# Splitting two attentions' weights in the feed-forwards ahead of them, with identity products and the first routed tiles' loads placed anew

## The chip, the cores and the metric

One Trainium2 chip, one of its cores. The metric is the device time of one execution of the whole program in microseconds (us), the median over several runs. The engines are TensorE (PE, with PEld for its weight loads), VectorE (DVE), ScalarE (ACT), GpSimd (POOL) and SyncE (SP, which here only issues transfers).

## What is computed

Eight sublayers in a row, each added to its input x (8 x 256 tokens of 256 numbers, all float32), with a context of 8 x 256 rows of 192:

```python
x = x + cosine_attention(layernorm(x), ctx, ...)       # L0 attention
x = x + moe_gelu(layernorm(x), ...)                    # L0: 2 shared + 16 routed experts, top 4
x = x + cross_attention(layernorm(x), ctx, heads=16)   # L1
x = x + bitlinear_silu(layernorm(x), ...)              # L1: ternary weights
x = x + cross_attention(layernorm(x), ctx, heads=8)    # L2
x = x + small_experts(layernorm(x), ...)               # L2: 8 experts, top 2
x = x + text_image_attention(layernorm(x), ctx, ...)   # L3: ternary weights, two attentions
x = x + routed_ffn(layernorm(x), ...)                  # L3: 8 experts, top 2

def cross_attention(x, context, Wq, Wk, Wv, Wo, bo):   # DIM_HEAD 64, SCALE 64 ** -0.5
    q, k, v = x @ Wq, context @ Wk, context @ Wv
    attn = softmax(q k^T * SCALE)                      # per head
    return (attn v) @ Wo + bo
```

## The kernel before

The program is a row of stages, each one block of five instruction streams (one per engine) that work against each other through semaphores. A block ends with a drain of every engine and a barrier, so no engine begins the next stage before the last has finished this one. The stages are `l0_cosine` (L380), `l0_ffn` (L648), `cross_attention` (L980) as l1x with 16 heads, `l1_ffn` (L1488), `cross_attention` as l2x with 8 heads, `l2_ffn` (L1711), `text_side` (L2039), `place_and_route` (L2377) and `routed_tiles` (L2639). Tokens stand in 16 tiles of 128; X holds them all in SBUF.

**Precision by splitting.** In the first feed-forward and both attentions a float32 product is made from two rounded parts: high = value rounded to F32R, low = value − high, and hi·hi + lo·hi + hi·lo on PE. The weights Wq, Wk and Wv are split once at the start of each attention block: ACT copies them to the high part (`hi_part`, L1210; the query's with the factor 64^-0.5), DVE makes the low part by one scalar_tensor_tensor (`lo_part`, L1301). In l1x an instruction covers 128x1024, in l2x 128x512, two for each weight. PE's first projection ("qk", 0) (L1103, L1106) waits for `wqk_lo` 4; the first value product ("v", 0) (L1131) for `wv_lo` 2. POOL zeroes the missing rows of wk and wv (L1444) and splits the context (`context(b)`, L1421 to L1426), adds the output bias to X (`bias`, L1441) and later divides by the row sums (L1434) and splits Wo (L1457). DVE's order at the start is: the norm's factors, all due `normalise(b)` (L1309, two tiles each), lows of Wq and Wk, `low_x(0)` (L1313), lows of Wv. PE's is: identity products, transposes of x(0) (L1092), identity products, qk(0).

**Where raw weights come from.** `K.raw` (8192 float32 columns) is shared: `load_attention_weights` (L917) fills it by SP. For l1x this stands in `l0_ffn`, behind the ternary quantiser's waits; for l2x at the end of l1x's SP stream.

**l0_ffn.** 18 experts by 4 chunks of 512 tokens are 72 units n. For each unit PE makes `hidden(n+1)` and `outputs(n)`, ACT the gelu (L819) and the high part (L823), DVE the low part (L855, `h − h_hi`, both in SBUF) and four scaled additions to X (L864). POOL splits each expert's weights four units ahead (L706 to L710) and between them makes ternary weights for later stages (`TernaryWeights.step`, L347 to L359). The last four units also make the next norm's statistics (L159).

**Identity products.** `keep_running(pe, K, bank, n)` (L98) issues n products of the identity, 128x256 in bfloat16, whose results are not used. The counts in the kernel before: l0_cosine 28 ahead of the sum; l0_ffn 26 at the start; the attentions 60 or 32 at the start and 44 behind x(0); l1_ffn 76; l2_ffn 28 at the start and 14 in `outputs(0, 0)`; routed_tiles 20.

**The last stage.** `routed_tiles` takes 39 tiles of 128 token slots. SP reads a tile's first row from `tile_row` (value_load) and loads its rows from DRAM (`slots`) into an area of XT; `place_and_route` before it writes the tables with DVE and scatters the tokens' rows with POOL's indirect transfers.

## Time and profile before

| | us |
|---|---|
| three runs | 1607.03, 1601.3, 1602.35 (median 1602.35) |
| the profiled execution | 1607.3 |
| its span, first to last instruction | 1605.6 |
| mean granted clock of TensorE | 0.974 |
| PE, DVE, ACT, POOL busy | 1473.8, 970.5, 772.7, 634.0 |

The granted clock is a share of 2.4 GHz: 1.00 is that, 0.50 is 1.2 GHz. All times below are from the span's start in the profiled execution. "Rows ready" is the end of the instruction that makes the last of the rows that the first transposes read; "products end" is where the identity products of the start give way to the first transposes.

| stage | begins | rows ready | products end |
|---|---|---|---|
| l0_cosine | 3.3 | 10.8 | none |
| l0_ffn | 68.7 | 71.8 | 74.0 |
| l1x | 315.0 | 319.2 | 323.8 |
| l1_ffn | 714.4 | 722.6 | 724.3 |
| l2x | 799.9 | 804.1 | 803.6 |
| l2_ffn | 1032.1 | 1035.5 | 1036.9 |
| text_side | 1138.2 | | |
| place_and_route | 1235.4 | | |
| routed_tiles | 1309.2 | | 1313.1 |

In a timeline row the columns are start, duration (of the whole group where there are several), engine, line, operation, output<-inputs, shapes, count, and in brackets the idle time before it with what ended it. L94 and L2414 as releaser are the barrier between two stages.

### The profile page before, as it was taken

The page shows a single profiled execution, that of the slowest core. Times are in us where ns is not written, and L with a number is a line of the kernel's source. Part 1 is how long each engine was busy: PE and PEld are TensorE (multiplying, and loading weights), DVE is VectorE, ACT ScalarE, POOL GpSimd, SP SyncE. Part 2 cuts the span into 40 slices and gives each one's busy share as a digit, 9 for nine tenths or more (in the row PEclk, how much of TensorE's full clock was granted, in tenths as well). Part 3 has the DMA queues.
Part 4 walks back from the last instruction along what each step waited for, and adds up shares of the span by engine and source line. Part 5 has one row for each costly group of instructions (what it writes and reads, how often), then busy time and mean ns, then how long its engine had stood idle before and what let it go on. Part 6 is the DMA issues. An engine that isn't in the chain of part 4 may idle for free. (4 is left out here: it accounts for less than half of the span.)

```text
span 1605.6 us, 29383 instructions
## 1 busy us (share of the span) xinstructions
PE 1473.8 (92%) x9850; PEld 1177.7 (73%) x9871; DVE 970.5 (60%) x2369; ACT 772.7 (48%) x1907; POOL 634.0 (39%) x828
## 2 busy tenths in 40 slices
PE   6799999899999999978899999789889859999997
PEld 4588888787777777755577767557565649999997
DVE  3768888865555555557866656455587634444443
ACT  2643444465555555526556565343558523434332
POOL 0138999463444443234365544001432432222212
PEclk9999999899999999999999999999999779999999
DMA  9000122309600000010000000100500842222220
GB/s 292 21 14 21 32 94 102 119 12 311 189 1 1 1 1 1 1 40 1 4 14 1 1 2 12 68 0 1 224 34 28 295 148 34 37 36 36 37 38 8
DMA packets 69266, 92.97 MB, mean 58 GB/s; under 512 B 7160, under 2 KB 60416, under 8 KB 68224
## 3 DMA queue, kind: packets, MB, share of 16 engines
q1 hardware_dynamic: 61968, 82.55, 16.4%
q0 software_dynamic: 7152, 8.55, 3.1%
q8 instruction: 83, 1.36, 0.3%
q14 instruction: 63, 0.52, 0.1%
HBM read 56.35 MB, written 35.63 MB: 57 GB/s over the span
## 5 line engine op out<-in xcount | busy, mean ns | idle before, releaser
L1434 POOL TENSOR_SCALAR XT<-XT,l1x_rs 128x256 f32<-128x256 f32 x256 | 118.1, 482 | 190.6 <-DVE l1x_rs L1318 190.6
L2699 POOL DMA_INDIRECT out_x<-XT x39 | 60.7, 1557 | 235.6 <-DVE XT L2795 233.6
L1322 DVE TENSOR_REDUCE l1x_nmax<-bank 128x2 f32<-128x512 f32 x128 | 87.4, 684 | 109.5 <-PE bank L1141 109.5
L1261 ACT ACTIVATE XT<-bank,l1x_nmax 128x256 f32<-128x256 f32 x256 | 118.9, 472 | 68.5 <-DVE l1x_nmax L1322 68.4
L2722 PEld LDWEIGHTS bank<-XT,l3x_qw 128*128 128x128 f32 x1248 | 145.3, 192 | 3.3 <-issue 0.7
L2722 PE MATMUL bank<-XT,l3x_qw 128*128 128x128 f32 x1248 | 145.8, 275 | 1.0 <-issue 0.5
L2734 PE MATMUL bank<-l3x_wd,CT 128*128 x624 | 141.0, 379 | 0.0
L1153 PE MATMUL bank<-ident,XT 128*128 128x128 f32 x768 | 120.8, 280 | 7.5 <-DVE l2x_pt L1329 3.5
L2734 PEld LDWEIGHTS bank<-l3x_wd,CT 128*128 128x128 f32 x624 | 115.6, 190 | 14.1
L864 DVE SCALAR_TENSOR_TENSOR X<-bank,l0f_gates,X 128x256 f32<-128x256 f32 x288 | 118.8, 473 | 3.0 <-PE bank L784 3.0
L100 PE MATMUL bank<-ident,identb 128*128 128x256 bf16 x616 | 85.8, 305 | 31.8 <-PEq L2414 17.5
L1153 PEld LDWEIGHTS bank<-ident,XT 128*128 128x128 f32 x768 | 84.3, 140 | 41.2 <-POOL XT L1434 20.9
L1329 DVE COPY l1x_pt<-bank 128x512 f32<-128x512 f32 x128 | 87.9, 686 | 30.5 <-PE bank L1153 30.5
L2770 ACT ACTIVATE CT<-bank,l3x_b 128x128 f32<-128x128 f32 x156 | 44.7, 368 | 125.4 <-PE bank L2722 125.3
L819 ACT ACTIVATE l0f_h<-bank 128x512 f32<-128x512 f32 x72 | 43.1, 599 | 127.7 <-PE bank L766 127.7
L100 PEld LDWEIGHTS bank<-ident,identb 128*128 128x128 bf16 x616 | 66.1, 109 | 47.5 <-issue 33.7
L2814 DVE TENSOR_SCALAR CT<-bank,l3x_b 128x128 f32<-128x128 f32 x156 | 44.1, 344 | 89.1 <-PE bank L2722 89.0
L782 PE MATMUL bank<-l0f_wdhi,l0f_hhi 128*128 128x256 f32 x288 | 83.0, 288 | 9.2 <-DVE l0f_hlo L855 9.1
L855 DVE TENSOR_TENSOR l0f_hlo<-l0f_h,l0f_hhi 128x512 fp32r<-128x512 f32 x72 | 67.6, 939 | 33.6 <-ACT l0f_hhi L823 33.2
L1434 POOL TENSOR_SCALAR XT<-XT,l2x_rs 128x256 f32<-128x256 f32 x128 | 59.1, 484 | 69.7 <-DVE l2x_rs L1318 69.2
L784 PE MATMUL bank<-l0f_wdhi,l0f_hlo 128*128 128x256 f32 x288 | 81.9, 284 | 0.0
L783 PE MATMUL bank<-l0f_wdlo,l0f_hhi 128*128 128x256 f32 x288 | 81.7, 284 | 0.0
(531 smaller groups left out, 3826.4 us busy)
## 6 DMA issues: line engine op xcount, KB each, us to landing
slots<-blank SPq DMA_DIRECT2D x9, 1987.5 KB, 21.4
l3x_wu<-in_L_ffn_W SPq DMA_DIRECT2D x8, 1024.0 KB, 12.9
l3x_wd<-in_L_ffn_W SPq DMA_DIRECT2D x8, 1024.0 KB, 8.8
XT<-slots SPq DMA_DIRECT2D x39, 132.5 KB, 2.1
l0f_wu<-in_L_ffn_upT SPq DMA_DIRECT2D x18, 128.0 KB, 2.1
l0f_wd<-in_L_ffn_downT SPq DMA_DIRECT2D x18, 128.0 KB, 2.2
X<-in_x SPq DMA_DIRECT2D x4, 512.0 KB, 5.5
l0x_later<-in_L_xattn_W_f1T SPq DMA_DIRECT2D x1, 2048.0 KB, 12.0
```

Of the source, the lines that this page charges most:

```text
L100: pe.matmul(bank[:, 0:2 * P], K.identb[:], K.ident[:].bitcast(BF16), start=True, stop=True)
L782: pe.matmul(y, h_hi[:, c % 2, w], wd_r[s][0][:], start=True, stop=False)
L783: pe.matmul(y, h_hi[:, c % 2, w], wd_r[s][1][:], start=False, stop=False)
L784: last = pe.matmul(y, h_lo[:, c % 2, w], wd_r[s][0][:], start=False, stop=True)
L864: dve.scalar_tensor_tensor(X[:, t, :], YB[c % 2 * 2 + j // 2][:, j % 2 * D:(j % 2 + 1) * D], gates[:, t, e:e + 1], X[:, t, :], ALU.mult, A ...
L1153: last = pe.transpose(tp[:, c:c + P], pr[n % 3][:, i, q, kt * P:(kt + 1) * P], K.ident[:])
L1261: act.activation(pr[n % 3][:, i, q, :], sc[(2 * n + i) % 3][:, q * S:(q + 1) * S], ACT.Exp, bias=nmax[:, n % 3, i, q:q + 1], accum_out=sum ...
L1322: dve.tensor_reduce(nmax[:, n % 3, i, :], sc[(2 * n + i) % 3][:].rearrange("p (q s) -> p q s", q=QT), AX, ALU.max, negate=True).then_inc(m ...
L1329: dve.tensor_copy(pt[n % 2][:, i, :], tp[:]).then_inc(pt_ok, 1)
L1434: pool.tensor_scalar(t, t, rs[:, n % 3, i, q:q + 1], 1.0, ALU.mult, ALU.mult).then_inc(norm_ok, 1)
L2722: last = pe.matmul(up_b[i % 2][half][:, j * P:(j + 1) * P], chosen[i % 2][:, k, m * P:(m + 1) * P], xT[i % 2][:, k, :], start=k == 0, stop ...
L2734: last = pe.matmul(y_b[i % 2][:, 0:D], hT[i % 2][:, m, :], wd[:, ds(e * HT + m, 1), :].rearrange("p a n -> p (a n)"), start=m == 0, stop=m ...
```

## The change

`load_attention_weights` gives way to a class `AttentionWeights`. One buffer `wqkv` of 8192 F32R columns, shared by both attentions, holds the high and low parts: Wq and Wk of l1x (Wv of l1x has a buffer of its own and is still split in l1x), all three of l2x. The query's weights are scaled in place by ACT, then copied to the high part; the low part is a subtraction on POOL in place of DVE's instruction. l1x's Wq and Wk are split in `l0_ffn`, l2x's weights in `l1_ffn`. In the attention block DVE now does `normalise(0)` and `low_x(0)` first and the other due tiles afterwards.

```diff
+class AttentionWeights:
+    def __init__(self, K, name):
+        self.parts = [[K.wqkv[:, (2 * i + part) * 2 * HD:...].rearrange("p (k n) -> p k n", n=HD) for part in range(2)]
+                      for i in range(min(3, WQKV // (4 * HD)))]
+        self.cuts = [slice(0, 1), slice(1, 2)] if HD == 1024 else [slice(0, 2)]
+    def scale_query(self, act, u):
+        act.wait_ge(self.raw_in[0], self.raw_n[0])
+        act.activation(self.raw[0][:, cut, :], self.raw[0][:, cut, :], ACT.Copy, scale=self.scale).then_inc(self.scaled, 1)
+    def high(self, act, i, u):
+        act.wait_ge(...)
+        act.activation(self.parts[i][0][:, cut, :], self.raw[i][:, cut, :], ACT.Copy).then_inc(self.hi_ok, 1)
+    def zero_rows(self, pool, i):
+        pool.memset(self.parts[i][1][HALF_C:P, 1, :].bitcast(F32), 0.0).then_inc(self.zeroed, 1)
+        pool.wait_ge(self.zeroed, i)
+    def low(self, pool, i, k):
+        pool.wait_ge(self.hi_ok, n * i + (k if n == 2 else 0) + 1)
+        pool.tensor_tensor(self.parts[i][1][0:rows, k, :], self.raw[i][0:rows, k, :],
+                           self.parts[i][0][0:rows, k, :].bitcast(F32), ALU.subtract).then_inc(self.lo_ok, 1)
```

In `l0_ffn` (POOL before its first split, POOL at its end, PE, ACT behind `hidden(n)`; N is 72):

```diff
+                if K.last >= 2:
+                    K.weights["l1x"].zero_rows(pool, 1)
                 pool.memset(gates[:, :, 0:NS], 1.0).then_inc(ones_ok, 1)
                 split(0)
...
+                    for i in range(2):
+                        for k in range(2):
+                            K.weights["l1x"].low(pool, i, k)
...
+                    if n == N - 1:
+                        keep_running(pe, K, bank[3], 15)
...
-                keep_running(pe, K, bank[4], 26)
+                keep_running(pe, K, bank[4], 30)
...
+                keep_running(pe, K, bank[3], 28)
...
+                    if K.last >= 2 and N - 10 <= n < N - 8:
+                        K.weights["l1x"].scale_query(act, n - (N - 10))
+                    elif K.last >= 2 and N - 8 <= n < N - 4:
+                        K.weights["l1x"].high(act, (n - (N - 8)) // 2, n % 2)
```

In `cross_attention` (PE, ACT, DVE, POOL):

```diff
-                keep_running(pe, K, tp, 60 if H == 16 else 32)
+                keep_running(pe, K, tp, 36 if H == 16 else 26)
...
                         if u == ("x", 0):
-                            keep_running(pe, K, tp, 44)
+                            keep_running(pe, K, tp, 14)
...
+                keep_running(pe, K, tp, 24 if H == 16 else 16)
...
                 norm.scalar(act)
-                act.wait_ge(K.raw_loaded, K.raw_needed[name])
-                for k in range(KD):
-                    hi_part(raw_q, wq, k, DH ** -0.5)
-                for k in range(2):
-                    hi_part(raw_k, wk, k)
+                if late_v:
+                    for k in range(2):
+                        weights.high(act, 2, k)
                 copy(("x", 0))
-                for k in range(2):
-                    hi_part(raw_v, wv, k)
...
-                for b in range(B):
-                    if turn_at.get(b, -3) - 1 <= -2:
+                normalise(0)
+                low_x(0)
+                for b in range(1, B):
+                    if turn_at[b] - 1 <= -2:
                         normalise(b)
-                for k in range(KD):
-                    dve.wait_ge(w_hi, k + 1)
-                    lo_part(raw_q, wq, k, wqk_lo, DH ** -0.5)
-                for k in range(2):
-                    dve.wait_ge(w_hi, 2 + k + 1)
-                    lo_part(raw_k, wk, k, wqk_lo, rows=HALF_C if k else P)
-                low_x(0)
-                for k in range(2):
-                    dve.wait_ge(w_hi, 4 + k + 1)
-                    lo_part(raw_v, wv, k, wv_lo, rows=HALF_C if k else P)
...
-                for w in (wk, wv):
-                    pool.memset(w[1][HALF_C:P, 1, :].bitcast(F32), 0.0).then_inc(w_zero, 1)
-                pool.wait_ge(w_zero, 2)
+                if late_v:
+                    weights.zero_rows(pool, 2)
                 context(0)
+                if late_v:
+                    for k in range(2):
+                        weights.low(pool, 2, k)
                 context(1)
                 bias(0)
```

In `l1_ffn` (POOL behind `lift_hidden(t)`, ACT at the end of tile t):

```diff
+                    for i in (1, 2):
+                        K.weights["l2x"].zero_rows(pool, i)
...
+                    if K.last >= 4 and 9 <= t < 15:
+                        K.weights["l2x"].low(pool, (t - 9) // 2, (t - 9) % 2)
...
+                    if K.last >= 4 and t == 2:
+                        K.weights["l2x"].scale_query(act, 0)
+                    elif K.last >= 4 and t in (4, 5, 6):
+                        K.weights["l2x"].high(act, t - 4, 0)
```

The other identity products: `l0_cosine` gets 34 ahead of its first transposes, 52 for 28 ahead of the sum and 10 behind it; `l1_ffn` 70 for 76; `l2_ffn` 14 more in `outputs(1, 0)`; `place_and_route` 44 at its end; `routed_tiles` 6 for 20. To make room, the ternary quantisers of the first two stages write over the raw values (`later`) and into XT in place of buffers of their own. The loads of the first two tiles' rows move from `routed_tiles` to the end of `place_and_route`'s SP stream, and the last table instruction of DVE signals SP:

```diff
+                sp.wait_ge(tables_ok, 1)
+                sp.wait_ge(scattered, 16 * NT * k)
+                first_tiles(sp)
                 sp.wait_ge(K.stored, 16 * NC)
...
-                load(0)
-                load(1)
                 sp.dma_start(b2.rearrange("p e d -> p (e d)"), b2_src.partition_broadcast(P)).then_inc(b2_in, 16)
-                for i in range(2, SLOT_TILES):
+                for i in range(tile_rows.EARLY, SLOT_TILES):
...
-                keep_running(pe, K, bank[7], 20)
+                keep_running(pe, K, bank[7], 6)
                 turn_input(0)
```

## Rows read from the trace of the kernel before

**Rows 1.** The page, part 1: busy time and share, instructions
```profile
PE 1473.8 (92%) x9850; PEld 1177.7 (73%) x9871; DVE 970.5 (60%) x2369; ACT 772.7 (48%) x1907; POOL 634.0 (39%) x828
```

**Rows 2.** Timeline of PE, 305 to 331: start, length, line, shape, idle before and releaser
```profile
315.08 8.84 PE L100 MATMUL bank<-ident,identb 128*128 128x256 bf16 x60 [4.18 <-PEq L94]
...
324.19 4.97 PE L100 MATMUL bank<-ident,identb 128*128 128x256 bf16 x44
328.92 0.49 PE L1103 MATMUL bank<-l1x_xhi,l1x_wqhi 128*128 128x256 f32 x2
```

**Rows 3.** Timeline of DVE, 303 to 331
```profile
317.08 2.17 DVE L1309 TENSOR_SCALAR XT<-X,l1x_small 128x256 f32<-128x256 f32 x2
319.17 2.89 DVE L1301 SCALAR_TENSOR_TENSOR l1x_wqlo<-raw,l1x_wqhi 128x1024 fp32r<-128x1024 f32 x2
321.99 3.99 DVE L1301 SCALAR_TENSOR_TENSOR l1x_wklo<-raw,l1x_wkhi 128x1024 fp32r<-128x1024 f32 x2
```

**Rows 4.** Timeline of PE, 798 to 815
```profile
799.97 3.65 PE L100 MATMUL bank<-ident,identb 128*128 128x256 bf16 x32 [1.84 <-PEq L94]
...
811.09 0.48 PE L1103 MATMUL bank<-l2x_xhi,l2x_wqhi 128*128 128x256 f32 x2 [1.50 <-DVE l2x_xlo L1313]
```

**Rows 5.** Timeline of DVE, 798 to 813
```profile
806.15 1.81 DVE L1301 SCALAR_TENSOR_TENSOR l2x_wqlo<-raw,l2x_wqhi 128x512 fp32r<-128x512 f32 x2
```

**Rows 6.** Windows: stretch, busy us of PE, PEld, DVE, ACT, POOL, granted clock
```profile
309.20:319.50 10.30, 6.12 (x31) 4.48 (x29) 8.89 (x26) 4.45 (x6) 4.22 (x5) 0.50 0.10 14
319.50:323.70 4.20, 4.20 (x41) 3.76 (x39) 4.20 (x3) 0.84 (x1) 4.04 (x3) 1.00 0.00 0
...
796.00:804.00 8.00, 4.80 (x41) 3.76 (x40) 4.48 (x14) 4.60 (x8) 3.75 (x5) 1.00 0.08 18
...
1097.70:1104.50 6.80, 6.80 (x25) 4.97 (x23) 1.69 (x10) 0.21 (x1) 2.16 (x4) 0.50 0.00 1
1295.70:1312.80 17.10, 3.53 (x17) 2.55 (x18) 3.21 (x8) 1.06 (x1) 6.72 (x7) 0.50 0.23 76
```

**Rows 7.** Groups by line and form, POOL subtractions and additions, mean ns
```profile
L1441 POOL TENSOR_TENSOR X<-X,l2x_bo 128x512 f32<-128x512 f32 x8 | 10.6, 1319 | 16.9 <-DVE XT L1309 16.8
...
L2628 POOL TENSOR_TENSOR X<-X,l3t_shift 128x1024 f32<-128x1024 f32 x4 | 9.3, 2375 | 26.1 <-DVE l3t_shift L2608 26.1
```

**Rows 8.** Line L1210, by source: ns of one, first and last start
```profile
L1210 ACT ACTIVATE l1x_wqhi<-raw x2: 1039/1040/1040, 316.5 to 317.4; 128x1024 fp32r<-128x1024 f32 x2
```

**Rows 9.** DMA issues from 268 to 296: KB each, us to landing
```profile
raw<-in_L_xattn_Wq SPq DMA_DIRECT2D x1, 1024.0 KB, 10.3
```

**Rows 10.** Timeline of ACT, 270 to 283
```profile
282.07 0.60 ACT L819 ACTIVATE l0f_h<-bank 128x512 f32<-128x512 f32 x1 [2.03 <-PE bank L766]
```

**Rows 11.** Timeline of DVE, 278 to 296
```profile
277.25 1.58 DVE L855 TENSOR_TENSOR l0f_hlo<-l0f_h,l0f_hhi 128x512 fp32r<-128x512 f32 x1 [0.56 <-ACT l0f_hhi L823]
...
283.37 0.69 DVE L855 TENSOR_TENSOR l0f_hlo<-l0f_h,l0f_hhi 128x512 fp32r<-128x512 f32 x1 [0.30 <-ACT l0f_hhi L823]
```

**Rows 12.** Timeline of POOL, 278 to 296
```profile
276.13 2.15 POOL L359 TENSOR_TENSOR l0f_back_q<-l0f_back_above,l0f_back_q 128x1024 bf16<-128x1024 bf16 x1
```

**Rows 13.** Timeline of PE at the seams and at two waits
```profile
17.92 2.08 PE L445 MATMUL bank<-CT,l0x_wt 128*128 128x512 f32 x2 [0.64 <-DMA CT<-in_ctxT]
...
68.72 5.42 PE L100 MATMUL bank<-ident,identb 128*128 128x256 bf16 x26 [1.75 <-PEq L94]
...
308.56 0.36 PE L782 MATMUL bank<-l0f_wdhi,l0f_hhi 128*128 128x256 f32 x1 [1.81 <-DVE l0f_hlo L855]
...
714.35 10.12 PE L100 MATMUL bank<-ident,identb 128*128 128x256 bf16 x76 [3.02 <-PEq L94]
...
1032.14 4.88 PE L100 MATMUL bank<-ident,identb 128*128 128x256 bf16 x28 [2.50 <-PEq L94]
...
1095.72 0.67 PE L1815 MATMUL bank<-l2f_b,l2f_weT 8*128 8x256 f32 x2 [1.65 <-DVE X L1987]
...
1309.27 4.03 PE L100 MATMUL bank<-ident,identb 128*128 128x256 bf16 x20 [17.54 <-PEq L2414]
```

139 lines of the change are left out of this document (85 added, 54 removed).

## The prediction, made before the changed kernel was run

> **What bounds the kernel now.** I read the page first: TensorE (PE) is busy 92% of the span [rows 1]. So time is gained only where PE waits, where it works at the low clock, or where it works on identity products while real work could have begun. The timeline at the seams of the stages shows the last. At the start of the first attention PE runs 60 and then 44 identity products, and the first projection of queries and keys starts at 328.92, 13.9 us after the block begins [rows 2]. In that time VectorE (DVE) normalises two tiles and then splits weights for 2.89 + 3.99 us before it may touch the queries' rows [rows 3]. The second attention has the same picture at half the width: its first projection is at 811.09, 11.2 us in [rows 4], with a split of 1.81 us for one weight and a like one for the next [rows 5]. The windows give the clock: 0.50 (1.2 GHz) in stretches behind seams, 1.00 (2.4 GHz) otherwise [rows 6].
>
> **The sum** is made against the profiled execution (1607.3 us, span 1605.6), which is 5.0 us over the median of 1602.35. A measurement of this kernel can tell about 0.5% (8 us) from no change.
>
> 1. *First attention's start: −7.3.* Without the splits DVE's normalise ends at 317.08 + 2.17 = 319.25 [rows 3]. Four transposes (0.6), ScalarE's (ACT) copy (0.6) and DVE's low part (0.7) put the first projection at about 321.4 against 328.92 [rows 2]: −7.5. The 36 products need 36 × 0.11 = 4.0 us at the full clock, so they end at 319.0, before the rows are there; 14 behind the transposes take 1.5, about the length of copy and low part. GpSimd (POOL) now also makes the value weights' low parts between its two first contexts, so its second context and the bias wait behind them: 2 × 2.4 us by the nearest row [rows 7], which makes the first value product at worst 2 us late. Bounds −8 and −5.
> 2. *Second attention's start: −4.9.* All four tiles were normalised ahead of the split (802.4 to 806.2); now two are, and the first projection falls at 804.3 + 1.9 = 806.2 against 811.09 [rows 4]. Two weights' splits leave the path [rows 5]. Bounds −5.5 and −4.
> 3. *Where the first attention's splits go: the first feed-forward, +2.3.* Six ACT instructions of 1.04 us [rows 8] stand behind the last units' activations. A unit takes 2.82 us, of which ACT works 1.23, so one instruction of 1.04 fits. But the first waits for Wq, issued at 271.75 and landing 10.3 us later [rows 9], at 282.05; it stands behind the activations of 278.8 and just ahead of those of 282.07 [rows 10], which are held for 1.0 us. I take +0.5 (0 to +1.1), PE having a unit in hand. POOL's four low parts of 128x1024, 2.375 us each by the nearest row of that size [rows 7], follow its last split at 293.84. DVE's subtraction with both inputs in SBUF (L855) takes 0.69 us alone and 1.58 beside a POOL subtraction: the one that starts at 277.25 ends at 278.83, and POOL's, of 2.15 us, ran from 276.13 to 278.28 [rows 11, 12]: DVE's waited for POOL's end and then ran. With low parts back to back a unit can't be shorter than 2.375 + 0.69 = 3.07 us, +0.25 for each of four; where DVE comes badly it is 0.9, as in rows 11. I take four of 0.45, +1.8. Bounds 0 and +7.6 (four whole low parts less DVE's half us of slack each). The Trainium skill, "SBUF — State Buffer", section "Who interferes with whom", says that a Vector instruction with two SBUF inputs contends with a GpSimd one that reads SBUF, and that the second to issue blocks until the first is done; the trace agrees, with 0.89 us lost behind 2.15. Taken strictly it allows the bad end of that bound.
> 4. *The first feed-forward's end: −0.9.* PE waits 1.81 us before the last output block, whose products then run at half clock from 309.2 [rows 13, 6]; 15 products (1.65 us) fill the wait. DVE's tail of statistics allows no end before 313.3 against 314.2. The 28 products behind the block end before that.
> 5. *Second attention's splits, in the second feed-forward: +0.5.* That stage is bound by DVE, whose work there reads PSUM or one SBUF tensor; ACT has gaps of 1.4 us between activations for its four instructions of 1.04, and POOL is idle for 43 us in all ahead of its quantisations. Each of six low parts of 128x512 at 1.32 [rows 7] can delay one of them. Bounds 0 and +1.5 by these gaps; with nothing hidden it is 4 × 1.04 + 6 × 1.32 = 12.1, which rival C takes.
> 6. *Seams.* In the table of seams the rows are ready before the identity products end. First feed-forward: 26 ran at half clock for 5.42 us from 68.72 [rows 13], and the transposes began at 73.98 though the rows were there at 71.8; at full clock 30 take 3.3. POOL's split of the first weights ends at 74.6 whatever PE does, so −1.0, and +0.3 for 10 products ahead of the seam: −0.7. Second: 76 took 10.12 from 714.35 [rows 13], rows ready at 722.6: −1.7, and +0.5 for 24 products that end behind DVE: −1.2. Third: 28 took 4.88 from 1032.14 [rows 13], rows ready at 1035.5: −1.0 (0 to −1.2).
> 7. *Third feed-forward's middle: −3.3.* PE waits 1.65 us until 1095.72 [rows 13]; from 1097.7 to 1104.5 the clock is 0.50 with PE never idle [rows 6]: 6.8 us at half speed, 3.4 lost. 14 products fill 1.54 of the wait. Bounds 0 and −3.4.
> 8. *The cosine's start: −1.5.* 34 products from 3.4 us on can raise the clock before the first rows, but the context lands only at 17.92 [rows 13], so PE then waits longer for it and the clock may fall again. From 17.92 to 32.8 PE works without a stop at half speed, 14.9 us, so the ends are 0 and −7.
> 9. *Last stage's start: −0.7.* 20 products took 4.03 us [rows 13] ahead of the first transposes; now 6 do, and the first tile's rows are loaded under POOL's drain. The real products come up to 2.4 us sooner, but at 0.50, where the clock rose at 1312.8 before [rows 6]. Bounds −2.4 and +1.
> 10. *At nothing:* the query scaled in place (the same ACT lengths, in a feed-forward); the ternary weights in other buffers; 44 products behind the routing, in a wait of 17.54 us [rows 13]; two loads of about 1 us to issue moved on SP's queue behind the stores, where nothing else is queued; SP's wait for the tables, whose last step ends before POOL's scatters. If POOL's drain didn't cover the loads, they'd cost 2 us, the bound of term 9.
>
> Sum: −7.3 − 4.9 + 2.3 − 0.9 + 0.5 − 0.7 − 1.2 − 1.0 − 3.3 − 1.5 − 0.7 = −18.7, so 1588.6 against 1607.3, or 1583.7 from the median. The 5 us between the runs shown are most likely clock; then the median run lacks some of the falls that 7 and 8 take back, and I put 1.3 back: 1585, −1.1%.
>
> **Rivals.**
> *A, the clock holds in the cosine (0.18).* Term 8 is −6 or −7: 1580. For it: PE's waits there are short once the context is in [rows 13]. Against: the wait for the context becomes some 3 us.
> *B, products don't hold the clock where they now stand (0.12).* PE idles of 1.81 and 1.65 us were followed by falls [rows 13, 6], one of 1.84 at 799.97 was not (1.00 from 796 to 804 [rows 4, 6]), so a short idle decides by its place. Fewer products then leave real work at half clock: terms 4, 6, 7 and 8 near nothing, 9 at +1, 1 at −5.5: sum about −6, 1596. The Trainium skill speaks for it, "TensorE: Matmul & The Clock Gate", Part 4: transpose-mode work does not count as busy in the same way. These are plain matmuls with the identity, and the row of 60 raised the clock by itself, 0.50 until 319.5 and 1.00 after [rows 2, 6]; the trace speaks against that rule for them.
> *C, slower (0.04).* The splits land on in-order queues in full stages. If each ACT instruction (10 × 1.04), the low parts by their bound (7.6) and the six of 1.32 are on the path, that is 25.9 in place of 2.8 counted, and the clock terms 4 and 6 to 9 (9.3) need not come: −18.7 + 23.1 + 9.3 = +13.7, 1616 from the median. It decides once the moved work costs over 21 us. Against it: ACT's wait for PE of 2.03 us before 282.07 [rows 10].
> *D, the splits' terms alone come (0.04):* −7.3 − 4.9 + 2.8 = −9.4, 1593.
> The forecast has 0.62.
>
> The range is 1576 to 1597: A less 4 for the bounds of 1 to 3, B plus 1. Faster by over 0.5% is below 1594.3: the forecast, A, most of D, a little of B: 0.85. Same 0.12, slower 0.03.
>
> **What would show it.** First projections some 6.3 us into both attentions; no DVE instruction that reads raw query, key or value weights; L855 slowed beside just four POOL low parts, the last of which ends before the stage does; one hidden activation about 1 us late at Wq's landing; clock 1.00 across the seams of term 6 and from 1097.7 to 1104.5; the middles of both attentions unchanged. I'd be wrong if units with an added instruction grew by its full length, or if falls of the clock only moved to the next real work.

## The result, and the profile after

The changed kernel takes 1598.06 us (median of seven runs, 1596.54 to 1602.27) against 1604.57 for the kernel before (seven runs, 1601.3 to 1610.65): a ratio of 0.996, 95% interval 0.9944 to 0.9975. That is 6.5 us where 17 were forecast (1585). The profiled execution has a span of 1600.5 us against 1605.6, so the profiles show 5.1 of these 6.5 and the stages can be set beside each other. Each column is one execution (the changed kernel's, at 1602.27 us, is the slowest of its seven), and what a stage does in other executions of the same code comes further down.

| stage | before | after | forecast change | change |
|---|---|---|---|---|
| l0_cosine | 65.4 | 65.9 | −1.2 | +0.5 |
| l0_ffn | 246.4 | 251.1 | +0.4 | +4.7 |
| l1x | 399.3 | 395.9 | −6.8 | −3.3 |
| l1_ffn | 85.6 | 85.6 | −1.2 | 0.0 |
| l2x | 232.2 | 229.6 | −4.9 | −2.6 |
| l2_ffn | 106.1 | 102.7 | −4.3 | −3.4 |
| text_side | 97.1 | 97.7 | 0 | +0.6 |
| place_and_route and routed_tiles | 370.2 | 368.7 | −0.7 | −1.5 |

(Stages are counted from the first busy instruction of one to that of the next; the last from 1235.4 and 1231.8 to the end.)

The page's row of busy time, which answers to [rows 1], says nothing of it:

```profile
PE 1478.2 (92%) x9953; PEld 1183.4 (74%) x9974; DVE 962.3 (60%) x2357; ACT 774.6 (48%) x1907; POOL 649.9 (41%) x840
```

Two stages come near what was forecast, the third feed-forward and the last. Both attentions give half of it, and the first feed-forward loses 4.7. I began with the first attention. DVE's timeline there:

```profile
321.30 1.30 DVE L184 TENSOR_TENSOR l1x_small<-l1x_small 128x16 f32<-128x16 f32 x1
322.88 0.25 DVE L186 RECIPROCAL l1x_small<-l1x_small 128x16 f32<-128x16 f32 x1 [0.28 <-ACT l1x_small L191]
323.17 0.25 DVE L187 SCALAR_TENSOR_TENSOR l1x_small<-l1x_small 128x16 f32<-128x16 f32 x1
323.45 3.31 DVE L1354 TENSOR_SCALAR XT<-X,l1x_small 128x256 f32<-128x256 f32 x2
328.14 0.69 DVE L1358 TENSOR_TENSOR l1x_xlo<-bank,l1x_xhi 128x512 fp32r<-128x512 f32 x1 [1.38 <-ACT l1x_xhi L1274]
```

In [rows 3] the normalise of two tiles took 2.17 us; it takes 3.31 now, and one of the norm's small instructions (L184, 128x16) takes 1.30, where it took 0.18 in the kernel before. POOL beside it:

```profile
320.26 0.95 POOL L976 MEMSET l1x_wvlo<- 64x1024 f32 x1 [11.31 <-POOLq L94]
321.29 1.28 POOL L1458 TENSOR_TENSOR l1x_chi<-CT,zero 128x512 fp32r<-128x512 f32 x1
322.65 0.74 POOL L1460 TENSOR_TENSOR l1x_clo<-CT,l1x_chi 128x256 fp32r<-128x256 f32 x1
323.46 0.73 POOL L1463 TENSOR_TENSOR l1x_chi<-CT,l1x_chi 64x256 fp32r<-64x256 f32 x1
324.27 2.34 POOL L983 TENSOR_TENSOR l1x_wvlo<-raw,l1x_wvhi 128x1024 fp32r<-128x1024 f32 x1
```

The instruction L184 starts at 321.30, just behind the start of POOL's context subtraction at 321.29, and ends at 322.60, when POOL's is done (322.57). In the kernel before two memsets of wk and wv stood in front of that context; one has gone with the change, the other is still there, and POOL's first context begins 1.0 us in where it began 1.9 us in. The normalise then runs beside POOL's third context instruction and the first low part of Wv, which the change had put there: its second tile starts with the low part, at 324.27, and ends at 326.76, 0.15 us behind the low part's end. PE shows what comes of it:

```profile
320.30 4.09 PE L100 MATMUL bank<-ident,identb 128*128 128x256 bf16 x36 [1.79 <-PEq L94]
326.82 0.66 PE L1146 MATMUL bank<-ident,XT 128*128 128x128 f32 x4 [2.43 <-DVE XT L1354]
327.31 2.52 PE L100 MATMUL bank<-ident,identb 128*128 128x256 bf16 x14
329.49 0.78 PE L1157 MATMUL bank<-l1x_xhi,wqkv 128*128 128x256 f32 x2
```

The first projection is 9.2 us behind the block's start, not 13.9 and not the 6.3 forecast, and it begins at the low clock: PE waited 2.43 us for the rows, and from 328.0 the windows have 0.50.

Windows of the changed kernel, with columns as in [rows 6]:

```profile
7.10:17.40 10.30, 5.01 (x30) 3.01 (x27) 9.46 (x38) 1.50 (x4) 0.00 (x0) 1.00 1.06 295
17.40:31.00 13.60, 13.01 (x39) 8.79 (x40) 1.58 (x5) 4.76 (x9) 0.00 (x0) 0.50 1.06 368
...
85.70:89.10 3.40, 3.40 (x16) 3.40 (x17) 2.00 (x3) 0.00 (x0) 0.95 (x1) 0.50 0.06 19
133.40:136.80 3.40, 3.40 (x14) 3.10 (x14) 2.92 (x8) 0.00 (x0) 0.00 (x0) 0.51 0.00 0
328.00:331.40 3.40, 3.40 (x19) 2.94 (x17) 0.69 (x1) 0.11 (x1) 3.24 (x4) 0.50 0.00 0
715.40:718.80 3.40, 2.56 (x24) 2.33 (x25) 1.24 (x9) 1.50 (x2) 1.48 (x3) 1.00 0.52 148
727.40:730.80 3.40, 2.84 (x7) 1.24 (x9) 0.00 (x0) 2.58 (x4) 3.29 (x7) 0.50 0.00 0
...
1094.00:1104.50 10.50, 10.39 (x59) 7.86 (x57) 4.43 (x18) 2.07 (x5) 2.15 (x4) 1.00 0.01 2
```

The other rows of this view say where the clock went: 1.00 from 1094 to 1104.5, as forecast; 1.00 early in the cosine, then 0.50 while it works behind the wait for the context; new falls at 85.7 and at 133.4 in place of those of the kernel before, at 66.9 and at 121.5; and at the second feed-forward's start the fall only moved, from the identity products (715.4) to the real ones (727.4). The seams of [rows 13] look as forecast in PE's timeline, a wait filled and transposes soon behind the products:

```profile
1031.42 3.22 PE L100 MATMUL bank<-ident,identb 128*128 128x256 bf16 x28 [0.95 <-PEq L94]
1034.86 1.09 PE L1820 MATMUL bank<-ident,l2f_xn 128*128 128x128 f32 x8 [0.22 <-DVE l2f_xn L1991]
```

and in the third feed-forward:

```profile
1092.99 1.69 PE L100 MATMUL bank<-ident,identb 128*128 128x256 bf16 x14
1094.80 0.67 PE L1866 MATMUL bank<-l2f_b,l2f_weT 8*128 8x256 f32 x2
```

In the second attention the norm is slowed in the same way: both memsets are gone from POOL's front, its context starts with the block, L179 takes 1.21 in place of 0.18, and the first projection comes 8.3 us in (11.2 before, 6.3 forecast). The first two normalises take 1.68 us, as before.

DVE's timeline at the second attention's start:

```profile
801.90 1.21 DVE L179 TENSOR_TENSOR l2x_small<-stats 128x16 f32<-128x16 f32 x1
803.04 0.17 DVE L180 TENSOR_TENSOR l2x_small<-stats 128x16 f32<-128x16 f32 x1
...
804.04 0.69 DVE L184 TENSOR_TENSOR l2x_small<-l2x_small 128x16 f32<-128x16 f32 x1
...
806.11 1.68 DVE L1354 TENSOR_SCALAR XT<-X,l2x_small 128x256 f32<-128x256 f32 x2
```

One profile doesn't price a stage. The experiments below leave several stages as they are in one kernel or the other, so each gives such a stage once more (us; for the second and third feed-forwards, all kernels with the old and with the new counts):

| stage | with the old code or counts | with the changed kernel's |
|---|---|---|
| l0_cosine | 65.4, 65.4, 65.2, 62.1 | 65.9, 65.9, 65.9, 63.7, 63.5, 63.4 |
| l0_ffn | 246.4, 246.7 | 251.1, 249.4, 249.4, 247.9 |
| l1_ffn | 85.6, 85.6, 85.7, 85.4 | five of 85.5 or 85.6, five of 84.0 or 84.1 |
| l2_ffn | 106.1, 106.2, 106.2, 102.9 | ten of 102.7 to 103.2 |

In the second feed-forward the two values part by the clock: the five of 85.5 and 85.6 each have a fall of 3.4 us that begins 10.9 to 11.7 us into the stage, the five of 84.0 and 84.1 have none. The table's +4.7 for the first feed-forward is the worst of four, and its +0.5 for the cosine lies within what the same code does.

### The profile page after: what moved, and what is told of

Read it like the earlier page. It is cut to its first block and busy times, and to the rows that moved or that the text cites. A ratio compares the mean times of both kernels' runs of the same rounds, so it can differ in the third digit from the quotient of the medians.

```text
span 1600.5 us, 29590 instructions
## 1 busy us (share of the span) xinstructions
PE 1478.2 (92%) x9953; PEld 1183.4 (74%) x9974; DVE 962.3 (60%) x2357; ACT 774.6 (48%) x1907; POOL 649.9 (41%) x840
## 5 line engine op out<-in xcount | busy, mean ns | idle before, releaser
L2804 PEld LDWEIGHTS bank<-l3x_wd,CT 128*128 128x128 f32 x624 | 115.6, 190 | 14.1
L100 PE MATMUL bank<-ident,identb 128*128 128x256 bf16 x719 | 91.2, 286 | 26.0 <-PEq L2466 15.3
L100 PEld LDWEIGHTS bank<-ident,identb 128*128 128x128 bf16 x719 | 72.3, 103 | 39.8 <-issue 28.6
L793 PE MATMUL bank<-l0f_wdhi,l0f_hhi 128*128 128x256 f32 x288 | 83.3, 289 | 11.5 <-DVE l0f_hlo L871 11.4
## 6 DMA issues: line engine op xcount, KB each, us to landing
l3x_wu<-in_L_ffn_W SPq DMA_DIRECT2D x8, 1024.0 KB, 13.9
```

The lines of the kernel that those rows point to most:

```text
L100: pe.matmul(bank[:, 0:2 * P], K.identb[:], K.ident[:].bitcast(BF16), start=True, stop=True)
L793: pe.matmul(y, h_hi[:, c % 2, w], wd_r[s][0][:], start=True, stop=False)
L2804: last = pe.matmul(y_b[i % 2][:, 0:D], hT[i % 2][:, m, :], wd[:, ds(e * HT + m, 1), :].rearrange("p a n -> p (a n)"), start=m == 0, stop=m ...
```

## The experiments

All are measured beside the kernel before, in five rounds; ratios are to it. Where two intervals overlap, a difference of medians between two of these kernels isn't settled by the times alone, and the profiles have to carry it. These theories stood at first. **C**: POOL's earlier subtractions block DVE's instructions for their whole length. **P or S**: the loss comes from the identity products placed anew, or from the splits in the first feed-forward.

### The two halves of the change alone

e1_products_old: the changed kernel with every count of identity products as before (13 places).

```diff
-                keep_running(pe, K, bank[7], 34)
-                keep_running(pe, K, bank[0], 52)
+                keep_running(pe, K, bank[0], 28)
...
-                keep_running(pe, K, tp, 36 if H == 16 else 26)
+                keep_running(pe, K, tp, 60 if H == 16 else 32)
```

> The changed kernel with every count of identity products as in the kernel before; splits and early loads stay. Theory P (the products placed anew cost more at the first feed-forward's start than they bring at other seams): the attentions' gains shrink, since 60 and 44 products hold x(0) and the first projection (first projection about 13 us in for 16 heads, 9 to 10 for 8 heads), the fall at 1097.7 is back (+3.4); against the kernel before a ratio of 0.998 to 1.000, 1601 to 1604. Theory S (the splits cost in the first feed-forward): the first feed-forward is still 4 to 5 us longer than before. If P holds it is at most 1.5 us longer.

Measured: 1610.15 us, ratio 1.0033 (1.0019 to 1.0047): slower than the kernel before, by more than either theory had. It is the cleanest look at the splits, because its falls of the clock at 66.9 and 121.5 are those of before to the tenth. In the first feed-forward its activations start within 0.11 us of those of before up to unit 62; unit 63 is 1.22 us late, then 0.49, 0.79, 0.80, 0.31, 0.32 and 0.81 at the end. So the splits cost 0.9 us there (0.81 + 0.11) and 0.4 more behind the last unit (term 3 had +2.3). Theory S falls. The stage is 1.2 us longer, not 4 to 5. In the attentions the products hold everything: the first projections come at 13.3 us, as expected, and at 11.3, where 9 to 10 were expected (the 44 products behind x(0) follow transposes at +6.1).

e2_products_new: the kernel before with the new counts alone.

> The kernel before with the new counts of identity products alone; the splits stay in the attentions. Theory P: its first feed-forward begins as in the changed kernel, with a late fall of the clock, and is 3 to 4 us longer than before; third feed-forward 3.4 us shorter; attentions unchanged or up to 2 us longer since PE idles and the clock falls ahead of the first projection; ratio 1.000, 1602 to 1606. Theory S: the first feed-forward is no longer than before, the sum is 5 us below it.

Measured: 1607.0 us, ratio 1.001 (0.9999 to 1.0021). The third feed-forward is 3.5 us shorter and the cosine 0.6; the first feed-forward is 0.8 longer, not 3 to 4, the second attention 1.9, because PE idles for 3.70 us before its first projection and that comes at half clock. So neither half is worth anything alone: the products fit only the shorter starts, and the splits only the new products. Theory P falls as a cause, too, but its part on falls that move stands.

This run also has a slow L184 in the second attention, with both memsets in place. First the kernel before (DVE, then POOL), then this run:

```profile
801.00 0.17 DVE L184 TENSOR_TENSOR l2x_small<-l2x_small 128x16 f32<-128x16 f32 x1
...
800.99 1.32 POOL L1421 TENSOR_TENSOR l2x_chi<-CT,zero 128x512 fp32r<-128x512 f32 x1
...
800.99 1.29 DVE L184 TENSOR_TENSOR l2x_small<-l2x_small 128x16 f32<-128x16 f32 x1
...
800.98 1.26 POOL L1427 TENSOR_TENSOR l2x_chi<-CT,zero 128x512 fp32r<-128x512 f32 x1
```

The two instructions start within 0.01 us of each other in both, and DVE's is held in one and not in the other. So the kernel before escaped the delay there by a hair.

### Whom POOL blocks

e3_context_waits:

```diff
                 if late_v:
                     weights.zero_rows(pool, 2)
+                pool.wait_ge(norm.coef_ok, 2)
                 context(0)
```

> The changed kernel, but POOL waits for the norm's last factor before its first context in both attentions. Theory C (without the old memsets POOL's context subtractions start 2 us earlier, onto DVE's small norm instructions, and block them): the norm's eight instructions take 2.0 us again in place of 3.1 and 4.2, first projections at +8.0 (16 heads) and +6.5 (8 heads) in place of +9.2 and +8.3, sum 2 to 3 us below the changed kernel, 1595 to 1596. Rival T (the late start comes from ScalarE's table load and its value copies, or from the clock): no change, 1598.

Measured: 1593.48 us, ratio 0.9927 (0.9908 to 0.9945). It is 4.6 us below the changed kernel by one wait more, and the two intervals (0.9908 to 0.9945, 0.9944 to 0.9975) only touch. The norm takes 2.0 and 1.9 us in the two attentions, the first projections are at +6.2 and +6.6 (better than expected: the forecast's 6.3). The attentions take 392.0 and 227.9 us, 7.3 and 4.3 below the kernel before, where 6.8 and 4.9 were forecast.

e6_context_behind_rows lets POOL wait until the first two tiles are normalised:

```diff
-                if late_v:
-                    weights.zero_rows(pool, 2)
+                pool.wait_ge(xn_ok, QT)
                 context(0)
                 if late_v:
+                    weights.zero_rows(pool, 2)
                     for k in range(2):
                         weights.low(pool, 2, k)
```

> The changed kernel, but POOL's first context, its memset and the value weights' low parts all wait until the first two tiles are normalised. Theory C: norm 2.0 us or less, the two normalise instructions 0.8 us in place of 3.3 and 1.7, first projections at about +5.5 in both, sum 4 to 6 us below the changed kernel, 1592 to 1594; the first value product in the 16-head attention waits up to 2 us more. Rival T: no change or 1 to 2 us slower, 1598 to 1600.

Measured: 1590.62 us, ratio 0.9916 (0.9901 to 0.9931), 7.4 us below the changed kernel. Its DVE timeline in the first attention, where nothing runs on POOL:

```profile
317.00 0.17 DVE L184 TENSOR_TENSOR l1x_small<-l1x_small 128x16 f32<-128x16 f32 x1
...
318.30 0.74 DVE L1354 TENSOR_SCALAR XT<-X,l1x_small 128x256 f32<-128x256 f32 x2
321.49 0.69 DVE L1358 TENSOR_TENSOR l1x_xlo<-bank,l1x_xhi 128x512 fp32r<-128x512 f32 x1 [2.46 <-ACT l1x_xhi L1274]
```

Two tiles are normalised in 0.74 us; it was 2.17 before, 3.31 in the changed kernel. The projections did not come at +5.5 but at +6.2 and +6.8, as in e3: PE's identity products now end later than the rows come (320.22 is +4.0, the rows are ready at +2.8). The rival T, that the table load or the clock is the cause, falls with both.

e12_memsets_late puts the same thing into the kernel before: its two memsets behind the first context, nothing else.

```diff
+                context(0)
                 for w in (wk, wv):
                     pool.memset(w[1][HALF_C:P, 1, :].bitcast(F32), 0.0).then_inc(w_zero, 1)
                 pool.wait_ge(w_zero, 2)
-                context(0)
```

> The kernel before with one edit: POOL's two memsets stand behind its first context in place of ahead of it, in both attentions. Nothing else is moved, so the clock and the splits are as before. Theory C: without 1.9 us (16 heads) and 1.0 us (8 heads) of memset ahead of them the context's subtractions start at once and block the norm: its eight instructions take 3.1 us in place of 2.0 (16 heads) and up to 4.2 in place of 2.3 (8 heads); the first projection comes up to 1 us later, or not at all later since the weights' splits set it. Rival T (the slow norm comes with the class AttentionWeights, not with the order on POOL): norm 2.0 and 2.3 us.

Measured: 1606.09 us, ratio 1.0006 (0.9991 to 1.002), so no time, the splits being the longer path there (first projections at +14.1 and +11.4); but the norm takes 3.7 and 3.6 us in place of 2.0 and 2.3, and that of the second attention shows the mark of the changed kernel:

```profile
797.39 1.21 DVE L179 TENSOR_TENSOR l2x_small<-stats 128x16 f32<-128x16 f32 x1
798.52 0.18 DVE L180 TENSOR_TENSOR l2x_small<-stats 128x16 f32<-128x16 f32 x1
...
798.83 0.59 DVE L182 TENSOR_SCALAR l2x_small<-l2x_small 128x16 f32<-128x16 f32 x1
...
799.53 0.69 DVE L184 TENSOR_TENSOR l2x_small<-l2x_small 128x16 f32<-128x16 f32 x1
```

L179, L182 and L184 take the 1.21, 0.59 and 0.69 us of the changed kernel, without any of its code, and in the first attention 1.29, 0.59 and 0.69. So the memsets had been a cover, if a chance one (e2_products_new). I had costed their removal at nothing.

e5_zero_rows_late asks the same of the first feed-forward, where the change had put a memset of 0.95 us ahead of everything on POOL:

```diff
-                if K.last >= 2:
-                    K.weights["l1x"].zero_rows(pool, 1)
                 pool.memset(gates[:, :, 0:NS], 1.0).then_inc(ones_ok, 1)
...
                 if K.last >= 2:
+                    pool.wait_ge(w_ok, 2 * E)
+                    K.weights["l1x"].zero_rows(pool, 1)
```

> The changed kernel with POOL's memset of wk's missing rows moved from the start of the first feed-forward to behind its last split. Theory C (a POOL instruction of 0.95 us also blocks DVE's norm here): the two norm instructions of 0.49 and 0.40 us take 0.17 each, the rows are ready 0.6 us sooner, ahead of POOL's first split, which lets the normalise instructions run at 0.41 in place of 0.82: first feed-forward 1 to 2 us shorter, 1596 to 1597. Rival: POOL's split waits for its transfer until 71.9 in both, and nothing changes, 1598.

Measured: 1595.44 us, ratio 0.9939 (0.9923 to 0.9956), 2.6 us below the changed kernel by the medians, with intervals that overlap. L182 and L183 take 0.18 and 0.17 us in place of 0.49 and 0.40. In the changed kernel (DVE, then POOL):

```profile
69.46 0.18 DVE L181 TENSOR_TENSOR l0f_ln_small<-stats 128x16 f32<-128x16 f32 x1
69.67 0.49 DVE L182 TENSOR_SCALAR l0f_ln_small<-l0f_ln_small 128x16 f32<-128x16 f32 x1
69.76 0.40 DVE L183 SCALAR_TENSOR_TENSOR l0f_ln_small<-l0f_ln_small 128x16 f32<-128x16 f32 x1
...
69.18 0.95 POOL L976 MEMSET wqkv<- 64x1024 f32 x1 [65.46 <-POOLq L94]
```

So a memset, which reads nothing, also delays DVE, but not each instruction: the TENSOR_SCALAR L182 waits for its end (70.13), and L183 ends with it. The three TENSOR_TENSOR ahead of them (L179 to L181), beside the same memset, take 0.15 to 0.18 us, and in e12_memsets_late a SCALAR_TENSOR_TENSOR beside a memset (L187, at 315.65) takes 0.18. The stage is 247.7 us in its profile. How much of this is the memset is not settled, since four executions of the changed kernel's code for this stage have 247.9 to 251.1: the falls come at 85.7 and 133.4 in the changed kernel's, at 78.4 and 122.8 in that of e3_context_waits (247.9). And the move had a price that I found only in e10_later_splits: from unit 68 to unit 69 this run, too, loses 1.6 us, with one DVE subtraction of 2.74 us beside POOL's first low part.

### What the identity products and the early loads bring

e8_seams_old is e6_context_behind_rows with the counts outside the attentions' starts as before.

> The kernel of e6_context_behind_rows with the identity products outside the attentions' starts as in the kernel before. Theory M (with the splits' gain no longer lost, the products at the seams bring what the third feed-forward shows, 3.4 us, and little else, since the fall of the clock only moves into the next real work): 3 to 4 us slower than e6_context_behind_rows, 1594 to 1595. Rival H (the forecast: each seam's products bring their part, 8 to 9 us in all): 1598 to 1600. Rival N (nothing, as in e2_products_new where they alone moved the median by +1.4): 1590 to 1592.

Measured: 1595.83 us, ratio 0.9935 (0.9916 to 0.9953): 5.2 us above e6_context_behind_rows by the medians, with intervals that overlap. That is between M (3 to 4) and H (8 to 9), nearer to M. In its profile, though, the third feed-forward is 102.9 us long with the old counts: here no fall of the clock came at PE's wait in its middle. So the 3.4 us of term 7 are lost in some executions and not in others, and these counts can't be priced by one profile each. Nor are the 5.2 us all theirs: Wq took 12.1 us to land in this execution, against 10.1 in e6_context_behind_rows, ScalarE waited 3.83 us for it, and the units 62 to 71 lost 3.4 us in place of 0.6.

e4_loads_late is the changed kernel with the first two tiles' loads back in the last stage.

> The changed kernel with the loads of the first two tiles' rows back at the start of the last stage, 6 identity products kept. If the early loads are what lets 6 products stand there: the first transposes wait for the transfer, 1309.2 + 1.2 + 2.5, about 2 us later than in the changed kernel, and the sum is 2 us longer, 1600. Rival: PE works at 0.50 there in both, and the later start means more time for the clock to rise: same, 1598.

Measured: 1600.8 us, ratio 0.9973 (0.9959 to 0.9987), 2.7 us above the changed kernel by the medians, again with intervals that overlap. PE waits for the transfer, and the last stage is 298.4 us in place of 295.2:

```profile
1299.76 1.44 PE L100 MATMUL bank<-ident,identb 128*128 128x256 bf16 x6 [12.47 <-PEq L2466]
1302.88 0.69 PE L2777 MATMUL bank<-ident,XT 128*128 128x128 f32 x2 [1.67 <-DMA XT<-slots]
```

In the changed kernel L2779 follows the six products at once (at +1.2). Term 9 had the mechanism and sized it too small.

e9_waits_filled is e6_context_behind_rows with products in four waits:

```diff
                     if c == 0:
+                        keep_running(pe, K, bank[7], 28)
                         pe.wait_ge(K.ctx_loaded, 48)
...
+                    if n in (0, 8, 10):
+                        keep_running(pe, K, YB[c % 2 * 2], 18 if n == 8 else 14)
```

> The kernel of e6_context_behind_rows with 28 products in the cosine's wait for the context (3.4 us at 14.6) and 14, 18 and 14 ahead of the output blocks 0, 8 and 10 of the first feed-forward (waits of 2.3, 2.4 and 3.2 us). If the early loss is the clock falling in these waits: clock 1.00 from some 7 us on until the end of the first feed-forward, first projection of the context at half its time, 6 us less in the cosine and up to 3.4 less in the feed-forward: 1582 to 1585. If the waits are bound by DVE (its selection and normalise) and the falls cost PE nothing there: cosine only, 1585 to 1587. Rival: the clock falls in the next wait all the same, 1590.

Measured: 1591.5 us, ratio 0.9904 (0.9886 to 0.9921), no gain over 1590.62. The cosine is 60.2 us long, 5.2 shorter than before, and the clock is 1.00 from 8.0 to 52.3: rival A's clock can be had. But the next stage gave 3.1 us of the 3.3 gained over e6_context_behind_rows back. PE waited 3.22 us at 70.4 for POOL's low part of the first rows and a fall of 6.8 us followed at 72.8; still, up to unit 62 the activations came 3.0 us ahead of those of e6_context_behind_rows. The loss is at the end: the units 65 to 71 were 3.1 to 3.6 us later than unit 62 (0.6 in e6_context_behind_rows at unit 71): ScalarE waited 2.73 us for Wq, PE then 1.84 us for DVE, and the clock fell at 284.4.

### The length of a POOL instruction

e10_later_splits is e6_context_behind_rows with e5's memset moved and ScalarE's six instructions one unit later (the first two of them here).

```diff
-                    if K.last >= 2 and N - 10 <= n < N - 8:
-                        K.weights["l1x"].scale_query(act, n - (N - 10))
+                    if K.last >= 2 and N - 9 <= n < N - 7:
+                        K.weights["l1x"].scale_query(act, n - (N - 9))
```

> The kernel of e6_context_behind_rows with the memset of e5_zero_rows_late moved as well, and ScalarE's six instructions of the first split one unit later (behind the units 63 to 68). The wait for Wq is then taken by no activation: unit 63 is not late (0.5 to 1.0 us in the units of the runs so far), the first feed-forward loses at most 0.5 us from unit 62 to 71, and with the norm's 0.6 us at its start the sum is 1 us below e6_context_behind_rows: 1589 to 1590. Rival: the low parts on POOL carry the cost and the units 65 to 69 are late by 0.5 to 1 us all the same: 1590 to 1591.

Measured: 1593.07 us, ratio 0.9925 (0.9904 to 0.9946), no better than 1590.62. The wait for Wq is gone as expected: against before, units 62 to 68 are all late by 1.00 to 1.03 us, no more than unit 61. But unit 69 is 1.65 us later at one stroke. One DVE subtraction did it, and POOL's beside it:

DVE:

```profile
293.11 1.18 DVE L871 TENSOR_TENSOR l0f_hlo<-l0f_h,l0f_hhi 128x512 fp32r<-128x512 f32 x1
...
296.16 2.75 DVE L871 TENSOR_TENSOR l0f_hlo<-l0f_h,l0f_hhi 128x512 fp32r<-128x512 f32 x1 [0.31 <-ACT l0f_hhi L835]
...
300.40 1.33 DVE L871 TENSOR_TENSOR l0f_hlo<-l0f_h,l0f_hhi 128x512 fp32r<-128x512 f32 x1
```

POOL, the first of the four:

```profile
295.98 2.38 POOL L983 TENSOR_TENSOR wqkv<-raw,wqkv 128x1024 fp32r<-128x1024 f32 x1
```

POOL's low part runs from 295.98 to 298.36. DVE's subtraction begins 0.18 us behind it and ends at 298.91, 0.55 after POOL's end: 2.75 us for 0.69 of work. This is the bad end of term 3's bound, on one unit. Moving the memset behind the last split had shifted the low parts by 1 us, to just ahead of DVE's subtraction; e5_zero_rows_late, where the memset alone is moved, has the same loss.

e11_all adds to it the products of e9_waits_filled and 26, 20 and 18 for 36, 26 and 14 in the attentions.

> e10_later_splits with the products of e9_waits_filled in the waits of the cosine and of the first feed-forward, and 26 and 20 products in place of 36 and 26 at the attentions' starts, 18 in place of 14 behind the first transposes (the rows are ready at +2.7, the products held them until +3.9 and +4.5). First projections at +5.7 in place of +6.1 and +6.7. If the products in waits hold the clock, the cosine stays at 60.3 us and the sum is 1585 to 1587; if what they bring is taken back by the first weights' transfer, which the first feed-forward waits for, 1588 to 1590.

Measured: 1589.1 us, ratio 0.9897 (0.9876 to 0.9917). The first projections are at +5.9 and +6.2, the cosine is 60.6 us; unit 69 is 1.65 us late again.

e13_low_pieces cuts POOL's low parts into pieces:

```diff
-        pool.tensor_tensor(self.parts[i][1][0:rows, k, :], ...
+        for a in range(0, cols, 256):
+            w = slice(a, a + 256)
+            last = pool.tensor_tensor(self.parts[i][1][0:rows, k, w], ...
```

> e11_all with every low part of the attention's weights on POOL made in pieces of 256 columns, so an instruction is 0.73 us in place of 2.4. Theory C, strictly (a DVE subtraction waits for the end of the POOL instruction that is under way): in e10_later_splits and e11_all one subtraction of the first feed-forward took 2.75 us and unit 69 was 1.65 us late; now none takes over 0.69 + 0.73 = 1.4 us, unit 69 is at most 0.5 us late, POOL's pieces last 12 to 15 us in all, and the first feed-forward is 1 us shorter: 1588 (the median of e11_all is 1589.1). Rival (the two share the port's throughput, so the pieces slow DVE as much as the whole): unit 69 is 1.5 us late again and DVE's subtraction takes over 2 us.

Measured: 1587.83 us, ratio 0.9896 (0.9879 to 0.9913). DVE's subtractions beside the 16 pieces:

```profile
292.01 1.10 DVE L874 TENSOR_TENSOR l0f_hlo<-l0f_h,l0f_hhi 128x512 fp32r<-128x512 f32 x1 [0.30 <-ACT l0f_hhi L838]
...
294.83 0.82 DVE L874 TENSOR_TENSOR l0f_hlo<-l0f_h,l0f_hhi 128x512 fp32r<-128x512 f32 x1
...
297.65 1.24 DVE L874 TENSOR_TENSOR l0f_hlo<-l0f_h,l0f_hhi 128x512 fp32r<-128x512 f32 x1 [0.43 <-ACT l0f_hhi L838]
```

and POOL:

```profile
291.83 12.97 POOL L989 TENSOR_TENSOR wqkv<-raw,wqkv 128x256 fp32r<-128x256 f32 x16
```

None takes more than 1.24 us, unit 70 is as late as unit 61 (to 0.01 us), and 16 pieces take 12.97 us where four whole ones took 10.84: POOL pays 2 us where nobody waits for it, DVE saves 1.5 where PE does. (In the first attention, where the pieces cut the low parts of wv, the profile has 393.3 us against 392.5.) The span is 1585.8 us, 14.7 below the profiled execution of the changed kernel; between the medians it is 10.2. By the medians it is the fastest kernel of the study, though its interval doesn't part it from e11_all.

## Why the prediction was wrong

Of the 18.7 us forecast against the profiled execution 5.1 came. Of the missing 13.6, 5.8 are in the attentions, 4.3 in the first feed-forward, 1.7 in the cosine and 1.2 in the second feed-forward. The first group is shown by experiments to be POOL blocking DVE; much of the rest goes with the clock and differs between executions.

*Terms 1 and 2 (−12.2; first projections 7.5 of it came).* The failed step is "Without the splits DVE's normalise ends at 317.08 + 2.17 = 319.25". It took the duration in [rows 3] for the instructions' own, and POOL's start for fixed. The rows were ready 6.5 us into the first attention, not 4.2. Two tiles take 0.74 us when POOL is quiet (e6_context_behind_rows), and the trace of before could have told: the median of this line's 32 instructions there is 0.41 us a tile. So the 2.17 already held POOL's blocking. Taking a memset from the front of POOL's queue moved a subtraction onto the norm, which cost 1.1 us at L184; and the low part of Wv, which the prediction prices only for what stands behind it on POOL, cost 1.1 at the normalise beside it. The last 0.6 are the 14 products behind the transposes, 2.52 us at the low clock in place of 1.5. In the second attention it is the norm alone, 4.2 us in place of 2.3. I had named the queue that got the low parts and not what the missing memsets would let start. With one wait more, e3_context_waits has the forecast's +6.3 (6.2 and 6.6) and is 4.6 us faster. (The parts of term 1 add up to 321.15 and not to 321.4, and its −7.5 stands in the sum as −7.3; neither matters here.)

*Term 3 (+2.3).* Right in kind and too high in size for this kernel: 0.6 us in the changed kernel's units and 0.4 behind them, 0.9 and 0.4 in e1_products_old, with unit 63 coming 1.0 and 1.3 us later than unit 62 at Wq's landing as described, and most of that made up one unit on. The wait for Wq is the part that can grow: in e8_seams_old and e9_waits_filled, where ScalarE waited 3.83 and 2.73 us for it, unit 63 came 2.8 and 1.7 us later than unit 62, more than the +0.5 (0 to +1.1) that I took. The bound on POOL's part was right: e10_later_splits lost 1.65 us on one unit by a shift of 1 us. The rule quoted there from the Trainium skill, "SBUF — State Buffer", section "Who interferes with whom", that the second to issue waits until the first is done, is what each of these rows shows (the 2.75 us above ends 0.55 behind POOL's end). I used it for L855 only. The same section says that tensor_scalar with a fast mode contends as well, which the normalise shows: 0.41 us for a tile alone, 2.50 for the one that began with POOL's low part.

*Term 4 (−0.9): nothing.* From the start of unit 71's activation to the next stage it is 9.9 us before, 10.3 after and 10.3 with the old products in e1_products_old. The failed step is that PE's half clock there was on the path. The fill worked (PE's wait is 0.17 us in place of 1.81, and the clock stays at 1.00), but DVE ends the stage: from its subtraction of 304.27 on it works without a pause until 314.17 in the kernel before. One of its subtractions beside a low part, at 305.59, takes 1.09 us in place of 0.67 in the changed kernel.

*Term 5 (+0.5): about 0.* Where the clock doesn't fall the stage takes 84.0 us with the splits in it, 1.6 less than before, and nearly the 1.7 that term 6 expects of the earlier rows is there; the ACT and POOL gaps hold the work.

*Term 6 (−2.9).* The failed step is that the clock was taken to stay at 1.00 once the seams were filled. In the second feed-forward the first transposes do come 1.6 us sooner (8.3 us in, not 9.9), but then the clock falls on the real products (727.4 to 730.8), and the third group of transposes is at +14.6, as before. That this is the clock and not a wait for rows, e4_loads_late and e5_zero_rows_late show, with the same code in this stage and no fall: POOL quantises the second chunk's rows at the same time (from +10.5 on), but the third group is at +13.0 and the stage takes 84.0 us, 1.6 less, as forecast. The fall on the next real work is what the prediction gives as a sign of being wrong. In the first feed-forward the rows were later, not sooner (4.3 us into the stage, where it was 3.1), because POOL's memset held the norm for 0.3 us and DVE's normalise then ran beside POOL's split, with 0.8 to 0.9 us a tile, and a wait of 2.32 us at 83.4 was followed by a fall. The units 3 to 9 came 2.85 us later than in the kernel before.

*Term 7 (−3.3): right* where the changed kernel is profiled; e8_seams_old shows that the loss it takes back isn't there in each execution.

*Term 8 (−1.5): +0.5.* The clock rose at 7.1 and fell again at 17.4 in the wait for the context, as described; 0.8 us came and 1.3 went when a fall then struck the last products (58.3). In three executions of the same code without that fall the cosine took 63.4 to 63.7 us; but the old code, too, took 62.1 once. So this term isn't settled either way. Rival A is possible with products in that wait (e9_waits_filled, 60.2 us), but it didn't pay.

*Term 9 (−0.7): −1.5.* Without the early loads the last stage is 3.2 us longer in the profile (2.7 by the medians), so they carry it: without them it would have been a loss.

Of the rivals, B has the nearest number (1596). That is partly luck: its mechanism, falls that come all the same, explains the second feed-forward and a part of the first, but not the attentions. C puts the loss on the moved work in full queues. But what blocked DVE in the attentions was, besides one low part, the old context subtractions, which start sooner although nobody had moved them. No rival named them.

What stays open: how much of the first feed-forward's 4.7 us is the change. The same code gave 247.9, 249.4 and 249.4 in other executions, so 1.5 to 4.7 us, and 3 us of it go by where the falls lie. The falls and POOL's blocking work together there: in the changed kernel PE waits 3.15 us until 132.9 for DVE, whose L646 takes 2.06 us (0.66 at 121.15) while POOL's L359 runs for 2.12, and the clock falls behind it; in e3_context_waits the fall comes earlier and the wait is 1.62 us. How the falls are spread over executions isn't known beyond these profiles.

## What to carry to other kernels

A duration in a trace is one beside its neighbours: before an instruction is costed, look whether its line has a shorter form elsewhere and who was busy then. When work is taken off a queue, what stood behind it starts earlier, and it must be asked what it lands on; here useless-looking memsets had kept a subtraction off the norm, by hundredths of a us in one place, and one wait in their stead gave back 4.6 us. An order that two queues need should be a wait and not the length of something else. Long instructions on POOL are best cut where DVE works on SBUF beside them: the pieces cost more on POOL's side and less on the path.

## What the runs showed of the hardware

A POOL subtraction delays DVE's small instructions by its whole rest: 128x16 took 1.21 and 1.30 us instead of 0.18. With starts 0.01 us apart the same pair was once held and once not. POOL's memset, which has no input, delayed a TENSOR_SCALAR of 128x16 (0.49 us instead of 0.18), but not the TENSOR_TENSOR beside it (0.18). DVE's normalise of a tile, 128x256, took between 0.41 and 2.50 us by what POOL did. The delay follows the length of POOL's instruction: at most 0.55 us over 0.69 with 0.73 us pieces, 2.06 with one of 2.38. And PE's clock fell after waits of 1.38, 1.65 and 2.40 us in one execution and not in another with the same code or counts in that stage. With the falls the first feed-forward moved by 3 us, the cosine by 2.5, the third feed-forward by 3.3 and the second by 1.6.
